# Five chunks of the first tile emptied early instead of four, all of unit 2's first layer placed before the flag is read, and image 1's gate steps moved up by one or two chunks

## The reference, cut to what matters

```
xn     = groupnorm(x)
scores = softmax(xn @ gate_w + gate_b);  top_v, top_i = top_k(scores, 2);  top_w = softmax(top_v)
coef[e, pixel] = sum over rank k of present[k, e] * top_w[k, pixel]
y_e    = relu(xn @ w1[e] + b1[e]) @ w2[e] + b2[e]        (384 -> 384 -> 384, four experts)
out    = x + sum over e of coef[e, pixel] * y_e
```

## Time and profile before

| what | value |
|---|---|
| three runs, median (lowest to highest) | 2469.34 us (2468.12 to 2470.34) |
| the profiled execution, its own time | 2469.91 us |
| its span (first to last instruction) | 2468.1 us |
| PE busy | 2449.9 us, 99% |
| DVE, ACT, POOL busy | 57%, 19%, 2% |
| mean granted TensorE clock | 0.999 of full speed |

### The profile page before, as it was taken

One profiled execution on the slowest core, in us unless ns is written; L12 is line 12 of the kernel. 1 busy time (PEld: TensorE's weight loads), 2 busy tenths in 40 slices (PEclk: granted clock), 3 DMA queues, 4 the chain that ended last, 5 costly groups with the idle time before them and its releaser, 6 DMA issues.

```text
span 2468.1 us, 27782 instructions
## 1 busy us (share of the span) xinstructions
PE 2449.9 (99%) x11372; PEld 2011.4 (81%) x11372; DVE 1413.7 (57%) x2952; ACT 465.6 (19%) x777; POOL 53.3 (2%) x36
## 2 busy tenths in 40 slices
PE   7999999999999999999999999999999999999999
PEld 6788888888888888888888888888888888888887
DVE  7765556556564556545564565556556564556443
ACT  3121111111111121111111121112111111121111
POOL 0000000000000000000000000000000000000000
PEclk9999999999999999999999999999999999999999
DMA  5223122221222213111321123121221222113110
GB/s 185 90 80 104 49 90 69 94 67 49 90 92 71 67 52 123 58 69 49 113 70 69 67 77 107 49 90 69 94 67 49 90 94 68 67 51 108 54 47 26
DMA packets 127520, 189.58 MB, mean 77 GB/s; under 512 B 16032, under 2 KB 80800, under 8 KB 127392
## 3 DMA queue, kind: packets, MB, share of 16 engines
q1 hardware_dynamic: 127392, 187.80, 22.5%
HBM read 146.03 MB, written 41.75 MB: 76 GB/s over the span
## 4 chain that ended last, share of the span: by engine, by line
PE 98%; DVE 1%; DMA 1%; issue 0%; ACT 0%; POOL 0%; SPq 0%; DVEq 0%; POOLq 0%
PE z_ps L432 16%; PE y_ps L451 16%; PE y_ps L452 16%; PE y_ps L453 16%; PE z_ps L434 16%; PE z_ps L433 16%; PE g_ps L300 1%; DMA rows<-rows_dram 0%; DMA rows_dram<-wrow 0%; DMA x_raw<-in_x 0%; DVE w_lo L386 0%; DVE h_lo L490 0%; DVE x_raw L278 0%; ACT h_hi L486 0%; POOL rstd L267 0%
## 5 line engine op out<-in xcount | busy, mean ns | idle before, releaser
L479 DVE SCALAR_TENSOR_TENSOR hid<-z_ps,b_sb,rows 128x512 f32<-128x512 f32 x584 | 436.7, 748 | 896.2 <-PE z_ps L434 892.9
L451 PE MATMUL y_ps<-h_lo,w_hi 128*128 128x512 f32 x1764 | 687.6, 390 | 4.2 <-DVE h_lo L490 4.2
L452 PE MATMUL y_ps<-h_hi,w_lo 128*128 128x512 f32 x1764 | 687.0, 389 | 0.0
L453 PE MATMUL y_ps<-h_hi,w_hi 128*128 128x512 f32 x1764 | 686.9, 389 | 0.0
L432 PE MATMUL z_ps<-x_lo,w_hi 128*128 128x512 f32 x1740 | 680.8, 391 | 0.0
L434 PE MATMUL z_ps<-x_hi,w_hi 128*128 128x512 f32 x1740 | 677.5, 389 | 0.0
L433 PE MATMUL z_ps<-x_hi,w_lo 128*128 128x512 f32 x1740 | 677.0, 389 | 0.0
L486 ACT ACTIVATE h_hi<-hid 128x512 fp32r<-128x512 f32 x588 | 368.6, 631 | 1554.4 <-DVE hid L479 1549.2
L490 DVE SCALAR_TENSOR_TENSOR h_lo<-hid,h_hi 128x512 fp32r<-128x512 f32 x588 | 401.0, 682 | 5.1 <-ACT h_hi L486 4.5
L451 PEld LDWEIGHTS y_ps<-h_lo,w_hi 128*128 128x128 f32 x1764 | 331.6, 188 | 74.4 <-issue 3.1
L432 PEld LDWEIGHTS z_ps<-x_lo,w_hi 128*128 128x128 f32 x1740 | 326.6, 188 | 76.0 <-issue 9.3
(11 more groups left out here) (88 smaller groups left out, 374.3 us busy)
## 6 DMA issues: line engine op xcount, KB each, us to landing
rows<-rows_dram SPq DMA_DIRECT2D x48, 1280.0 KB, 6.1
x_raw<-in_x SPq DMA_DIRECT2D x62, 588.0 KB, 6.0
res<-in_x SPq DMA_DIRECT2D x18, 768.0 KB, 5.5
out<-res SPq DMA_DIRECT2D x17, 768.0 KB, 4.3
rows_dram<-wrow SPq DMA_DIRECT2D x32, 98.0 KB
w_in<-in_w SPq DMA_DIRECT2D x3, 576.0 KB, 9.9
res<-in_x SPq DMA_DIRECT2D x2, 744.0 KB, 4.9
out<-res SPq DMA_DIRECT2D x2, 744.0 KB, 4.1
```

Source lines behind the costliest of these rows:

```text
L451: nc.tensor.matmul(y, w2_hi[:, e, k, ms], h_lo[:, slot], start=first, stop=False)
L452: nc.tensor.matmul(y, w2_lo[:, e, k, ms], h_hi[:, slot], start=False, stop=False)
L453: ins = nc.tensor.matmul(y, w2_hi[:, e, k, ms], h_hi[:, slot], start=False, stop=last)
L479: nc.vector.scalar_tensor_tensor(hid[:, q % HIDS], z_ps[:, q % ZB], b1_sb[:, e, k:k + 1], coef, ALU.add, ALU.mult).then_inc(scaled, 1)
```

## The change

More of the change, by code:

```diff
@@ L26 @@
 HIDS = 3
-EARLY = 4
+EARLY = 5
 WARM = 9
@@ L112, in conv_moe @@
         w2_in = [res_flat[:, NJ * T:NJ * T + slab], slab_of(hid_flat, 0), w_in[:, 1], w_in[:, 2]]
-        early = rows[:, 1, 1:1 + EARLY]
+        early = rows[:, 1, 0:EARLY]
         st6 = sb("st6", [P, NJ * HALVES, 6])
@@ L414, in mm1_early, with mm1 @@
                         ins.then_inc(z_ready, 1)
-        def mm1(pe, u, chunks=range(NK)):
+        def mm1(pe, u):
             t, e = divmod(u, E)
@@ L421, in mm1 @@
                 pe.wait_ge(main.xlo_ready, parts_to(t))
-            for k in chunks:
+            for k in range(NK):
                 q = NK * u + k
@@ L460, in relu_early @@
             act.wait_ge(z_ready, q + 1)
-            nc.scalar.activation(early[:, q], z_ps[:, q, 0:T], ACT.Relu,
+            nc.scalar.activation(early[:, q], z_ps[:, q % ZB], ACT.Relu,
                                  bias=b1_sb[:, q // NK, q % NK:q % NK + 1]).then_inc(early_done, 1)
@@ L663, in _ @@
                     gate_logits(dve, main, 1, lk)
-                if q == 8:
                     gate_top2(dve, main, 1, lk)
                     gate_gap(dve)
-                if q == 9:
+                if q == 8:
                     gate_weights(dve, 1, lk)
                     gate_coefs(lk, wrow_ready)
+                if q == 9:
                     biases(lk)
@@ L718, in _ @@
             weight_hi(1, 3)
+            relu_early(act, 4)
             split_x_hi(act, 1, 0)
@@ L832, in _ @@
             mm1_early(pe, 1, range(NK), ("hh", "hl", "lh"), counts=True)
-            mm1_early(pe, 2, range(2), ("hh", "hl", "lh"))
+            mm1_early(pe, 2, range(NK), ("hh", "hl", "lh"))
             pe.wait_ge(flag_ready, 1)
@@ L844, in _ @@
                         gate_product(pe, main, n, n % SLOTS)
-                if 0 < u < UNITS - 1:
-                    mm1(pe, u + 1, chunks=range(2 if u == 1 else 0, NK))
+                if 1 < u < UNITS - 1:
+                    mm1(pe, u + 1)
                 if u == 2:
```

## The result

| | before | after |
|---|---|---|
| median of 22 runs (lowest to highest) | 2469.40 us (2467.85 to 2471.12) | 2465.31 us (2464.44 to 2466.41) |
| profiled execution, span | 2469.91, 2468.1 us | 2466.06, 2464.3 us |

The ratio of the times is 0.9983, with a 95% interval of 0.9977 to 0.9989: 4.1 us faster, less than 0.2%. The forecast was 2464.7, with a range of 2463.2 to 2467.2 and 0.53 for "within 0.2%". The number by itself does not part the forecast from rival D (2465.8), since the measured time lies halfway between the two; the trace has to do that.

What follows compares the result with a forecast made beforehand. PE bound the kernel, matmuls back to back except two 2.10 us waits. 2.04 + 1.48 + 1.13 + 0.25 = 4.9 us off 2469.91 gave 2465.0, or 2464.4 by the median; forecast 2464.7, range 2463.2 to 2467.2.

Steps and rivals of the forecast that it cites:

- rival D: New wait before unit 2's third mm2 chunk eats the shorter chain: gain about 3.9 us, 2465.8; chance 0.11.
- chunk 8 out of the loop, and the clock: Nine matmuls moved into PE's idle time before mm2 of unit 0: 2.04 us, plus 1.48 for avoided half clock.
- gate product's end to the write of the rows: Image 1's top two directly behind the exponential, no longer behind scale(9) and h_lo(8): 1.13 us off the chain.
- PE's new wait for h_lo(8): Before the third chunk of mm2 of unit 2, PE waits 0.9 us, from 58.95 to 59.85.
- scale(12) to add_product: DVE busy without a break up to tile 1's second layer: 8.97 us, moving with the landing of the rows.
- The term of the load: Tile 1's coefficient rows: second load issued some 2.5 us behind disturbs the first less, 0.25 us gained (bounds 0, 0.4).
- The clock term: At mm2 of unit 0: filling PE's idle time avoids half clock, 1.48 us saved (from 0 to 1.64).
- rival A: Clock gain at mm2 of unit 0 not real, or mostly not paid before: gain 3.4 us, 2466.2; chance 0.13.
- Rival B: PE's branch before mm2 of unit 0 has a hidden cost that holds it back: gain 1.4 us, 2468.2; chance 0.07.
- Rival C: Clock falls in the new wait at 58.95 and stays lower: slower, 2472 with 15 us of half clock; chance 0.03.

Runs made afterwards that it cites:

- the warm execution of before: Profiled execution of a repeat of the kernel before, no edit, at full clock throughout; that repeat's median 2468.73 us, ratio 0.9998.
- the filler: The kernel before plus eight matmuls whose result nobody reads, on PE between the flag and mm2 of unit 0; median 2468.71 us, ratio 0.9997.
- the second profile: Profile from a repeat of the changed kernel, no edit, on the chip of later experiments; that repeat's median 2465.18 us.

## Why the prediction was right, and where its sizes were off

Each step from the start of h_lo(0), as forecast and as the profile after shows it:

| step | forecast | measured |
|---|---|---|
| chunk 8 out of the loop, and the clock: gate product's end | 3.52 sooner | 24.19 to 20.70: 3.49 |
| gate product's end to the write of the rows | 1.13 less | 7.63 to 6.49: 1.14 |
| issue of the load to scale(12) | 0.25 less | 6.51 to 6.42: 0.09 |
| PE's new wait for h_lo(8) | 0.9 | 0.69 listed, 0.85 from the due start 59.84 to 60.69 |
| scale(12) to add_product | 8.97, unchanged | 8.96 |
| sum | 4.9 | 4.73 |

The medians show 4.1, and the sum can be brought to that: 0.6 less because four in ten runs of the kernel before did not pay the 1.6 between the levels, and 0.2 less for the load.

**The mechanism.** It held in every step: the 2.04 us of matmuls went into idle time, the top two follow the exponential by 0.26 us, the new wait stands where it was named, and it does not add to the time since the rows end at the same moment. mm2 of unit 3 goes on at 73.11, 0.05 behind the end of h_lo(11). A single part gives less than its share: with chunk 8 alone 1.8 in the medians, with the gate steps alone 1.6, and 4.1 with both. Compared warm with warm, the parts roughly add up: 2.0 and 1.2 to 1.4 alone, 2.9 together. What only both bring is that no run is cold any more, as no idle stretch of 2 us is left.

**The term of the load was mis-sized.** I took 0.25 us off, reasoning that a second load 2.5 us behind disturbs less. The runs with it 2.6 behind show 6.4 to 6.7 from issue to scale(12), no less than with it 1.2 behind (6.5 to 6.6). Only held back or 3.4 us behind does the first reach 6.2 to 6.3. The term is about 0.

**The clock term is an average, not a constant.** Against a cold execution the 1.48 is right (1.43 by the warm execution of before, 1.50 by the filler). But 30 of 77 runs of the kernel before did not pay it, and against these the gain is 2.9. The median of before stands for a mixture. The prediction put rival A (2466.2) at 0.13 as a matter of yes or no, where it is the case in four runs of ten of the kernel before. So my step from 2465.0, worked out from a cold execution, to 2464.7 had no ground. The clocks of the three runs with the median of 2469.34 are not on record; whatever they were, a median that may hold warm runs says nothing of the changed kernel, which is warm in all. The rest of the difference to 2465.3 is of the size of the load's 0.25.

What decides whether a run is cold is not shown beyond this: behind waits of 1.5 to 2.1 us before mm2 of unit 0 the clock stayed up (1.48), fell at about the restart (2.10), or fell one microsecond after PE had begun again (1.91), and behind waits of 2.1 to 2.2 us before unit 3's last chunk it stayed up three times and fell once. The Trainium skill, "TensorE: Matmul & The Clock Gate", section "What's actually happening", says that the window of the clock gate runs free of the program. The runs agree: neither the place nor the length of the wait decides alone.

**Rival B fell.** After the change the branch is executed late:

```profile
L836 PEldq COMPARE_BRANCH  x1: 230/230/230, 32.8 to 32.8; - x1
```

It ends at 33.0, and PE goes on at 36.00 without a gap. A hidden cost behind the branch is 3.0 us at most, and none of it shows. What sets the 36.00 is PE itself: h_lo(0) ended at 35.67, and PE came 0.33 behind it instead of 0.14, since the early gate product had taken 1.67 us and not 1.20. Its matmuls took 534 ns at the longest and 329 at the shortest, the ratio of 632 to 389 ns between half and full clock at 36 to 39 us before the change; so it began at half clock, although the granted clock is recorded as 1.00 there. Such start-up jitter was hidden by 2.1 us of idle time before; in this execution 0.2 us of it shows, in the second profile none. The Trainium skill's rule in "Runtime: NRT & Kernel Launch", section "Instruction fetch mechanics", is not tested by this, as nothing tells whether the target had to be fetched.

**Rival A fell:** the clock read 1.00 at 36.00, and the first nine matmuls of mm2 of unit 0 took 2.06 us. **Rival C fell:** the clock was 1.000 in all 33 runs, in spite of the new wait. **Rival D fell:** h_lo(8) began 4.26 behind the gate product's end, for 4.27 forecast, and PE had no wait left before unit 3's last chunk, where the rows and its own way end within 0.1 us of each other.

## What to carry to other kernels

Where the engine that bounds has two idle stretches, count the clock with both: one filled stretch may only hand the cold start on to the next. Before a forecast of a tenth of a per cent is set against a median, look whether the runs of the kernel lie on two levels of the clock, and forecast the mixture. And where two paths end together, as PE's wait and the rows here, only an edit that shortens both pays: moving h_hi(8) and h_lo(8) into the idle time ahead of the logits did, for 1.2 us; the coefficients straight behind the gap brought perhaps 0.4 more.

## What the runs showed of the hardware that was not expected

- With two idle stretches of PE of about 2 us the mean granted clock was 0.999 in 47 of 77 runs of the kernel before. With none longer than 0.7 us after the start (in both profiles) it was 1.000 in all 33 runs of the changed kernel.
- The clock can fall after PE has resumed: with the gate steps alone mm2 of unit 0 began at 35.09 with matmuls 0.23 apart, and they were 0.43 apart from 36.10 on.
- At the very start the granted clock is recorded as 1.00 while the durations of matmuls say half clock (534 ns for 329). So the mean clock of a run does not count the first cold stretch.
- A broadcast load of 1280 KB took 6.4 to 6.7 us where a second was issued 1.2 or 2.6 us behind it, and 6.2 and 6.3 where it was alone or the second came 3.4 behind. A lone load also took 6.4 once, so the disturbance is likely and its size is open.
- The start of h_lo(0) lay between 32.99 and 34.98 in ten profiled executions with almost the same opening. What follows takes the same time whenever it starts, so this goes into the run time whole, and single runs cannot tell apart kernels that differ by less.
